# Expert rows divided 112 + 64 instead of 88 + 88, four result rows summed on TensorE, and the front of the middle stage done tile by tile, in a mixture-of-experts block on one Trainium2 core

## The reference

```python
x = x + attn(_layernorm(x), ...)            # 16 heads, 4 KV heads, causal, soft cap 50
x = x + ffn(_layernorm(x), ...)             # first expert stage
x = x + recur(_layernorm(x), Wa, Wx, ba, bx, Lam)
x = x + ffn(_layernorm(x), ...)             # second expert stage, same weights

def ffn(x, gate, Wg, Wu, Wd, Sg, Su, Sd):   # E = 64 experts, M = 176, capacity 96, top 6
    scores = softmax(x @ gate.T)            # the 3 best of 8 groups, then the 6 best experts
    slot = expert * 96 + min(place within the expert, 95)
    buf = zeros(E * 96, 256).at[slot].set(x[token]).reshape(E, 96, 256)
    g, u = einsum('ech,emh->ecm', buf, Wg), einsum('ech,emh->ecm', buf, Wu)
    out = einsum('ecm,ehm->ech', silu(g) * u, Wd)
    y = sum over the 6 choices of out[slot] * weight
    return y + silu(x @ Sg.T) * (x @ Su.T) @ Sd.T

def recur(x, Wa, Wx, ba, bx, Lam):          # h[t] = a[t] * h[t-1] + sqrt(1 - a[t]**2) * i[t] * x[t]
    r, i = sigmoid(x @ Wa.T + ba), sigmoid(x @ Wx.T + bx)
    a = exp(-8 * softplus(-Lam) * r)
    ...
```

## Time and profile before

| | |
|---|---|
| runs | 1285.45, 1286.99, 1289.58 us; median 1286.99 us |
| profiled execution | 1283.71 us, span 1281.9 us |
| busy, share of the span | PE 77%, PEld 46%, DVE 41%, ACT 57%, POOL 33% |
| stages | attention 0 to 623 us, first experts 692 to 845, middle 845 to 1085, second experts 1087 to 1240, end to 1282 |

### The profile page before, as it was taken

How to read it: one execution, slowest core, us unless ns; L and a number is a source line. 1 busy time by engine, 2 the same in 40 slices (tenths; PEclk the granted TensorE clock), 3 DMA queues, 4 the chain that set the end, 5 groups by cost and what they waited for, 6 DMA issues and landing times.

```text
span 1281.9 us, 18696 instructions
## 1 busy us (share of the span) xinstructions
PE 985.2 (77%) x6520; PEld 594.9 (46%) x6520; DVE 523.4 (41%) x1532; ACT 728.9 (57%) x960; POOL 423.7 (33%) x408
## 2 busy tenths in 40 slices
PE   4886868778887788787554999955587863999973
PEld 3633323322332323222334999943344442999962
DVE  7744431156221233230441333337776741333327
ACT  2285989999999999999101444414434400344420
POOL 3100000000222003234043565530098985556550
PEclk9878888998999998999686999976698976999985
DMA  9990000000111001100583999748133434899947
GB/s 352 394 393 31 1 1 1 1 17 1 42 47 37 17 16 60 39 20 6 148 254 92 292 295 289 177 118 273 50 116 117 123 109 106 243 293 284 261 72 305
DMA packets 94927, 176.11 MB, mean 137 GB/s; under 512 B 13119, under 2 KB 46880, under 8 KB 94833
## 3 DMA queue, kind: packets, MB, share of 16 engines
q1 hardware_dynamic: 58416, 130.55, 30.4%
q0 software_dynamic: 23616, 28.44, 10.4%
q10 hardware_dynamic: 12800, 15.93, 4.5%
HBM read 107.30 MB, written 83.72 MB: 149 GB/s over the span
## 4 chain that ended last, share of the span: by engine, by line
PE 32%; DVE 5%; DMA 3%; issue 3%; SPq 2%; POOL 2%; ACT 2%; DVEq 1%; POOLq 0%; ACTq 0%
PE PS L1323 13%; PE PS L1334 8%; PE PS L1261 4%; PE PS L1393 2%; PE PS L1310 2%; POOL expert_in L307 2%; SPq L1116 1%; DMA spare_space<-expert_out 1%; DMA normed<-xp 1%; SPq L1117 1%; PE PS L1246 1%; DMA XE<-expert_in 1%; PE PS L1270 1%; DMA expert_out<-ob,yidx 1%; POOL expert_out L1209 1%
## 5 line engine op out<-in xcount | busy, mean ns | idle before, releaser
L307 POOL DMA_INDIRECT expert_in<-xp,didx x192 | 192.9, 1005 | 621.7 <-ACT PR L684 483.9
L679 ACT ACTIVATE PR<-PS 128x1024 f32<-128x1024 f32 (+3 forms) x320 | 275.4, 935 | 55.7 <-PE PS L578 40.7
L684 ACT ACTIVATE PR<-PR 128x2048 f32<-128x2048 f32 (+3 forms) x160 | 272.4, 1705 | 0.0
L1209 POOL DMA_INDIRECT expert_out<-ob,yidx x128 | 180.6, 1411 | 148.2 <-ACT ob L1502 108.3
L587 PE MATMUL PS<-PR,V 128*32 128x512 f32 (+3 forms) x1280 | 164.8, 590 | 80.4 <-ACT PR L684 80.3
L575 PE MATMUL PS<-QT,KT 96*128 96x512 bf16 (+3 forms) x640 | 177.5, 372 | 19.8 <-ACT PR L679 16.9
L1740 DVE SCALAR_TENSOR_TENSOR gta<-gth,PS 88x192 f32<-88x192 f32 x128 | 44.8, 350 | 193.6 <-ACT gth L1492 193.6
L575 PEld LDWEIGHTS PS<-QT,KT 96*128 96x128 bf16 x640 | 59.3, 103 | 130.3 <-ACT PR L679 89.7
L1492 ACT ACTIVATE gth<-PS 88x192 f32<-88x192 f32 x128 | 41.7, 326 | 107.8 <-PE PS L1323 107.8
L1323 PEld LDWEIGHTS PS<-XT,spare_space 128*88 128x88 f32 x960 | 92.5, 164 | 8.8 <-issue 2.6
L1502 ACT ACTIVATE ob<-PS,wslot 96x256 f32<-96x256 f32 x128 | 60.1, 469 | 61.9 <-PE PS L1334 59.6
(11 more groups left out here) (257 smaller groups left out, 1355.3 us busy)
## 6 DMA issues: line engine op xcount, KB each, us to landing
spare_space<-in_wgu SPq DMA_DIRECT2D x60, 352.0 KB
expert_out<-zero SPq DMA_DIRECT2D x2, 8256.0 KB, 50.4
expert_in<-zero SPq DMA_DIRECT2D x2, 7776.0 KB, 39.3
XE<-expert_in ACTq DMA_DIRECT2D x32, 486.0 KB, 9.8
WGU<-in_wgu SPq DMA_DIRECT2D x44, 352.0 KB
spare_space<-expert_out SPq DMA_DIRECT2D x24, 512.0 KB, 6.1
spare_space<-in_wd SPq DMA_DIRECT2D x60, 176.0 KB
shared_space<-in_wgu SPq DMA_DIRECT2D x24, 352.0 KB
```

The costliest lines, as they stand in the source:

```text
L307: pool.indirect_dma_start(out=buf_d[f], out_offset=bass.IndirectOffsetOnAxis(ap=didx[b][:, r, j:j + 1], axis=0), in_=xp[b][:, r, :], in_of ...
L679: act.activation(PR[:, n % 3, 2 * pr:2 * pr + 2, cols(c, s):CW], PS[:, S0 + 2 * pr:S0 + 2 * pr + 2, cols(c, s):CW], ACT.Tanh, scale=1.0 / ...
L684: act.activation(PR[:, n % 3, :, lo:CW], PR[:, n % 3, :, lo:CW], ACT.Exp, scale=SOFT_CAP).then_inc(exp_done, 1)
L1209: pool.indirect_dma_start(out=y_d[f], out_offset=bass.IndirectOffsetOnAxis(ap=yidx[:, n % 4, j:j + 1], axis=0), in_=ob[:, i % EU, :], in_o ...
```

## The change

Three things are changed together. (1) The 176 middle rows of an expert are divided into 112 + 64. Gate a and up a are products with 112 weight columns; the last 64 rows of gate and of up are one product with 128 weight columns. That is six matmuls for each expert instead of eight. DVE's second instruction becomes two of 96 columns each, and the down weights are loaded by two DMAs (112 rows and 64 rows of 1 KB) instead of one of 88 rows of 2 KB. (2) The four result rows are summed on PE: the overflow product of each tile stays open and four products with the identity matrix add the four rows; DVE adds only the sum to X. The rows are awaited and released tile by tile. (3) Turning and copying of rows goes tile by tile (`turn_rows`, `turn_recur`: PE turns tiles 2 and 3 when ACT has copied tiles 0 and 1), and the order in the middle loop changes: `place` ahead of the sums on PE, and for c = 1 `slots` and `destinations` ahead of `recur_inputs` on DVE, with the statistics of two chunks taken one after the other. The last chunk of the end is added and stored in two halves.

```diff
-MH = M // 2
+MA = 112
+MB = M - MA
# loads on SP
-                sp.dma_start(wd, wd_d[e]).then_inc(loaded, 16)
+                sp.dma_start(wd[:, 0, :], wd_d[e, 0:MA, :]).then_inc(loaded, 16)
+                sp.dma_start(wd[0:MB, 1, :], wd_d[e, MA:M, :]).then_inc(loaded, 16)
# results on SP
-                if f == 0 and c:
-                    sp.wait_ge(results_free, c)
                 for r in range(CT):
                     i = CT * c + r
+                    if f == 0 and c:
+                        sp.wait_ge(result_psum, i - CT + 1)
# PE
-                    for j in range(4):
+                    for j, at, width in ((0, 0, MA), (2, MA, MA), (1, 2 * MA, 2 * MB)):
                         for hh in range(CH):
-                            last = pe.matmul(PS[0:MH, 4 + e % 2, j * CAP:(j + 1) * CAP], wgu[:, hh, MH * j:MH * (j + 1)],
+                            last = pe.matmul(PS[0:width, 4 + e % 2, j * CAP:(j + 1) * CAP], wgu[:, hh, at:at + width],
                                              XT[:, h % 2, e % EH, hh, :], start=(hh == 0), stop=(hh == CH - 1))
-            def overflow_rows(c):
+            def sum_rows(c):
                 ...
                 for r in range(CT):
-                    last = pe.matmul(PS[:, S0 + r // 2, (r % 2) * C:(r % 2 + 1) * C], WovT[...], O95[:], start=True, stop=True, ...)
-                last.then_inc(ov_psum, 1)
+                    acc = PS[:, S0 + r // 2, (r % 2) * C:(r % 2 + 1) * C] if c else PS[:, (S0, S0 + 1, A0, A0 + 1)[r], 0:C]
+                    pe.matmul(acc, WovT[...], O95[:], start=True, stop=False, ...)
+                    pe.wait_ge(y_ld[r], 16 * (c + 1))
+                    for j in range(NACC):
+                        last = pe.matmul(acc, const("ident"), GB[:, r, j * C:(j + 1) * C], start=False, stop=(j == NACC - 1), ...)
+                    last.then_inc(result_psum, 1)
             ...
+                    if r >= 2:
+                        pe.wait_ge(rowsT_ready, CT * n + r - 1)
             # the loop
                 if c < NC:
                     gates(c)
-                if c + 2 < NC:
-                    overflow_rows(c + 2)
                 if c:
                     place(k)
+                if c + 2 < NC:
+                    sum_rows(c + 2)
# ACT: one copy of each tile instead of one of all four
-                act.activation(xnT[:], PS[:, T0:T0 + 2, :], ACT.Copy).then_inc(rowsT_ready, 1)
+                for r in range(CT):
+                    act.wait_ge(rowsT_psum, CT * n + r + 1)
+                    act.activation(xnT[:, :, r * P:(r + 1) * P], PS[:, T0 + r % 2, ...], ACT.Copy).then_inc(rowsT_ready, 1)
# DVE, experts
-                    dve.scalar_tensor_tensor(ha[:, e % 2, :, :]..., bank[:, 2 * CAP:4 * CAP], 0.5, gta[:], ALU.mult, ALU.mult)
+                    dve.scalar_tensor_tensor(ha[:, e % 2, 0, :], bank[0:MA, 2 * CAP:3 * CAP], 0.5, gta[:, 0:CAP], ALU.mult, ALU.mult)
+                    dve.scalar_tensor_tensor(ha[0:MB, e % 2, 1, :], bank[MB:2 * MB, CAP:2 * CAP], 0.5, gta[0:MB, CAP:2 * CAP],
+                                             ALU.mult, ALU.mult).then_inc(act_ready, 1)
# DVE, statistics of chunk 0, tile by tile
+                        if (before, after) == (0, None):
+                            dve.wait_ge(result_psum, r + 1)
+                            added = dve.tensor_tensor(X[:, r, :], X[:, r, :], PS[:, (S0, S0 + 1, A0, A0 + 1)[r], 0:C], ALU.add)
             def add_results(c):
-                ...
-                dve.tensor_tensor(xc, xc, GB[:, :, 0:C], ALU.add).then_inc(results_free, 1)
+                dve.wait_ge(result_psum, CT * (c + 1))
+                dve.tensor_tensor(xc, xc, PS[:, S0:S0 + 2, :]..., ALU.add).then_inc(ov_added, 1)
# DVE, the loop
-                if c:
+                if c == 1:
+                    statistics(None, 0)
+                    statistics(2, None)
+                elif c:
                     statistics(c + 1 if c + 1 < NC else None, c - 1)
                 ...
-                if c == 1:
-                    add_results(3)
                 if c:
                     shift(k)
                     choose(k)
+                if c == 1:
+                    slots(k)
+                    destinations(k)
                 if c < NC:
                     recur_inputs(c)
                 if c + 2 < NC:
-                    add_overflow(c + 2)
+                    add_results(c + 2)
-                if c:
+                if c >= 2:
                     slots(k)
                     destinations(k)
# DVE combine_late and SP: the last chunk in two halves of two tiles, each stored when it is added
-                for r in range(CT):
+                for lo, hi in ((0, CT),) if c < NC - 1 else ((0, 2), (2, CT)):
```

More of the change, by code:

```diff
@@ L1048, in hybrid_kernel @@
         WD_space = keep("WD_space", [P, EU * 2 * C])
[L1049 removed]
+        WD = WD_space[0:MA, :].rearrange("p (e m c) -> p e m c", e=EU, m=2)
         XE = keep("XE", [CAP, 2, EH, RW])
         XT = keep("XT", [P, 2, EH, CH, CAP])
[L1052 to L1054 removed]
+        gth = keep("gth", [MA, 2, 2 * CAP])
+        gta = keep("gta", [MA, 2 * CAP])
+        ha = keep("ha", [MA, 2, 2, CAP])
         ob = keep("ob", [CAP, EU, C])
@@ L1077, in expert_weights @@
             loads = f * len(range(x, E, RING)) + e // RING + 1
-            return wgu, wd, ring_ld[x], 32 * loads
+            return wgu, wd, ring_ld[x], 48 * loads
         def last_user(x):
@@ L1178, in _ @@
                 results(1, c)
-            for c in range(NC):
+            for c in range(NC - 1):
                 sp.wait_ge(combined, c + 1)
                 sp.dma_start(x_rows[:, CT * c:CT * (c + 1), :], X[:, CT * c:CT * (c + 1), :]).then_inc(out_stored, 16)
-            sp.wait_ge(out_stored, 16 * NC)
+            for half in range(2):
+                i = CT * (NC - 1) + 2 * half
+                sp.wait_ge(combined, NC + half)
+                sp.dma_start(x_rows[:, i:i + 2, :], X[:, i:i + 2, :]).then_inc(out_stored, 16)
+            sp.wait_ge(out_stored, 16 * (NC + 1))
         @block.gpsimd
@@ L1332, in down @@
                     wd = expert_weights(f, e)[1]
-                    for m in range(2):
-                        last = pe.matmul(PS[0:CAP, 6 + e % 2, 0:C], ha[:, e % 2, m, :], wd[:, m, :],
+                    for m, width in enumerate((MA, MB)):
+                        last = pe.matmul(PS[0:CAP, 6 + e % 2, 0:C], ha[0:width, e % 2, m, :], wd[0:width, m, :],
                                          start=(m == 0), stop=(m == 1))
@@ L1375, in turn_recur @@
                     pe.wait_ge(xt_ready, NH)
[L1376 to L1379, removed]
+                for r in range(CT):
+                    if r < CT - 1:
+                        pe.wait_ge(recur_tile, (CT - 1) * c + r + 1)
+                    else:
+                        pe.wait_ge(xr_ready, c + 1)
+                    if r >= 2:
+                        pe.wait_ge(xrT_ready, CT * c + r - 1)
+                    for h in range(CH):
+                        at = (r // 2) * C + h * P
+                        last = pe.transpose(PS[:, T0 + r % 2, at:at + P], xr[:, r, h * P:(h + 1) * P], const("ident"))
+                    last.then_inc(xrT_psum, 1)
             def gates(c):
-                pe.wait_ge(xrT_ready, c + 1)
+                pe.wait_ge(xrT_ready, CT * (c + 1))
                 if c:
@@ L1414, in _ @@
             experts(0)
-            overflow_rows(0)
-            overflow_rows(1)
+            sum_rows(0)
+            sum_rows(1)
             turn_recur(0)
@@ L1453, in turned_rows @@
                 n = k - K0
-                act.wait_ge(rowsT_psum, n + 1)
                 if n:
                     act.wait_ge(shared_psum, n * SC)
-                act.activation(xnT[:], PS[:, T0:T0 + 2, :], ACT.Copy).then_inc(rowsT_ready, 1)
+                for r in range(CT):
+                    act.wait_ge(rowsT_psum, CT * n + r + 1)
+                    act.activation(xnT[:, :, r * P:(r + 1) * P],
+                                   PS[:, T0 + r % 2, (r // 2) * C:(r // 2 + 1) * C].rearrange("p (h n) -> p h n", h=CH), ACT.Copy)\
+                       .then_inc(rowsT_ready, 1)
             def scores(k):
@@ L1491, in gate @@
                         act.wait_ge(act_ready, i - 1)
-                    act.activation(gth[:, e % 2, :], PS[0:MH, 4 + e % 2, 0:2 * CAP], ACT.Tanh, scale=0.5).then_inc(gate_tanh, 1)
+                    act.activation(gth[:, e % 2, :], PS[0:MA, 4 + e % 2, 0:2 * CAP], ACT.Tanh, scale=0.5).then_inc(gate_tanh, 1)
                 def out(e):
@@ L1555, in turned_recur @@
                     act.wait_ge(gates_psum, 4 * c)
-                act.activation(xrT, PS[:, T0:T0 + 2, :], ACT.Copy).then_inc(xrT_ready, 1)
+                for r in range(CT):
+                    act.wait_ge(xrT_psum, CT * c + r + 1)
+                    act.activation(xrT[:, :, r * P:(r + 1) * P],
```

(2 more changed lines are left out.)

111 lines of the change are left out of this document (51 added, 60 removed).

## The result

The changed kernel took 1317.21 us (median of 4 runs, 1314.43 to 1323.63), the kernel before 1286.22 in the same comparison. The ratio is 1.025, with a 95% interval of 1.021 to 1.029: slower by some 31 us, and far outside the predicted range of 1256 to 1288. The profiled execution took 1315.19 us (span 1313.4), 31.5 us more than before's.

A forecast was written before the change was run, and what follows sets the result against it. PE bounds the expert stages, a chain of waits the middle stage's front, POOL its rest. Gains of 1.0 + 5.9 + 1.2 + 5.9 = 14.0 us take 1287.0 to 1273.0 us; range 1256 to 1288.

The forecast's parts named there:

- the down product takes 0.87 us in 4, 217 ns each: Expert stages: time of an expert's down product, 4 instructions with 256 moving columns, read from the trace before the change.
- the second rival: Expert stages: wide loads cost 110 ns on average, each stage at -1.0 to +1 us; 1286 us, chance 0.16.
- The load as the pace: Expert stages: weight loads bound gate and up, 8 at 97 ns and 4 at 111 ns, 1.22 us against 1.32.
- loads hidden: Rival for the expert stages: 96 moving columns stay the pace, each stage gains 19 to 21 us; 1245 us, chance 0.12.
- the division does nothing: The second rival's title: wide loads in the expert stages cancel the gain; 1286 us, within 0.3%, chance 0.16.
- DVE and DMA in the expert stages: Expert stages: DVE's extra instruction costs about 0.2 us behind the last expert only, the third weight DMA nothing.
- The front of K0: Before the first experts: tile-wise turning and copying lets `shift` move earlier; 1.0 us gained, bounds 0 and 1.2.
- The middle stage, k = 4: Front of the middle stage: sums at 8.7 us a chunk, row numbers for k = 4 come 1.2 us early.
- The rival with the lower clock: Middle stage: the clock stays at 1.2 GHz through the front, chunk 2's sums end 30 us later; 1303 us, chance 0.10.
- It holds, barely: Middle stage: k = 5 comes 1.9 us late against a slack of 3.4 - 1.2 us, so POOL need not wait.
- the slack of 3.4 us: Middle stage before the change: k = 5's row numbers are written at 964.76 us, POOL takes them at 968.37 us.
- The end, about nothing: End: two halves cost DVE about 0.6 us more, the last store is half as long; nothing, within 0.5 us.

The follow-up runs named there:

- pad_all: pad_down with the overflow product's WovT and O95 also padded with zeros from 64 to 128 rows; 1274.15 us, ratio to before 0.9911.
- pad_down: The changed kernel with the second down product zero-padded from 64 to 112 rows and its two weight transfers made one again; 1280.08 us, ratio to before 0.9954.
- pad_all_again: The same kernel as pad_all, timed again in a second comparison; 1278.45 us, ratio to before 0.9938.
- rows_88_72: The kernel before with the second down product summed over 72 of its 88 rows, nothing else changed; 1283.05 us (one run).
- division_padded: The kernel before with only the 112 + 64 division and the second down product zero-padded to 112 rows; 1272.23 us, ratio to before 0.9899.

## Why the prediction was wrong, step by step

- **The step that failed: "the down product takes 0.87 us in 4, 217 ns each" was carried over unchanged to a product over 64 rows.** The sum priced the wider loads of gate and up, and nothing for the fewer rows of the second down product. It takes 1.03 us, and gate and up behind it pay a second time, 1.40 instead of 1.22. That is 0.34 us an expert against a gain of 0.10: a loss of 0.24, or 15 us a stage, where the gain of 5.9 was forecast. My bounds did not hold it either: the second rival came nearest ("something that L1246 does not show"), but bounded it by 111 ns for every instruction, at +1 us, and looked at columns, not rows.
- **The trace of before had a row for it.** This is PEld's timeline at the end of the gates of c = 0, where the overflow product, with 64 rows, followed them:

```profile
881.20 0.19 PEld L1393 LDWEIGHTS PS<-spare_space,wab 128*128 128x128 f32 x1 [0.24 <-issue]
881.63 0.19 PEld L1393 LDWEIGHTS PS<-spare_space,wab 128*128 128x128 f32 x1 [0.24 <-issue]
882.57 1.59 PEld L1354 LDWEIGHTS PS<-O,WovT 64*128 64x128 f32 x8 [0.76 <-issue]
```

  The usual gap under products of 512 columns is 0.24 us; the load with 64 rows had 0.76, "<-issue". That the rows make the difference is shown by pad_all, where WovT has 128 rows at the same place and the gap is the usual one:

```profile
877.37 0.19 PEld L1368 LDWEIGHTS PS<-O,WovT 128*128 128x128 f32 x1 [0.24 <-issue]
```

  It was one crossing for eight instructions there, cheap enough to be overlooked. The change put it at every tile and at every expert.
- **The load as the pace, right.** The estimate of 97 and 111 ns, 1.22 us for 12 instructions, is what pad_down shows, to 0.01 us; the split into 97 and 111 ns was not measured by itself. With the down product padded, the stages gain 6.1 and 7.0 us (pad_down) against 5.9. The rivals "loads hidden" (1245 us) and "the division does nothing" (1286 us) are both out. The Trainium skill's rule for the duration of a load (TensorE: Matmul & The Clock Gate, section LDWEIGHTS) would have given 9 us a stage; the rows' own pace was nearer.
- **DVE and DMA in the expert stages, right.** DVE's second step lasts 0.26 us, and PE waited for it 4 times (2.4 us, in the list above). The lists of L1337 and L1348 name no DMA among what PE waited for.
- **The front of K0, right in size.** From ACT's small instruction at the end of `lambdas` to the first send it takes 26.4 us before (626.01 to 652.36), 25.0 in pad_all (626.43 to 651.46), 24.8 in pad_all_again and 24.0 in the changed kernel: 1.4 to 2.4 us less, against 1.0 forecast and a bound of 1.2.
- **The middle stage, k = 4: right but for the same cost.** I had the sums at 8.7 us a chunk and k = 4 sent 1.2 us earlier. Sums of 10.2 us made it 2.0 us later. With WovT padded it is sent 1.7 us earlier (79.7 against 81.4 us). The rival with the lower clock did not come: the clock in 845 to 928 us rose from 0.64 to 0.84.
- **"It holds, barely" for k = 5, wrong, crossings or not.** POOL waited 1.34 us, in the changed kernel and in both traces of pad_all. The row numbers of k = 5 came 37.7 us after those of k = 4 before and 41.4 us after them in pad_all: 3.7 us more, where the sum had 3.1 (1.2 + 1.9). And the slack of 3.4 us left out that POOL starts a send 0.9 us after its row numbers are written (918.35 to 919.22 us in pad_all). k = 4 to 7 took 151.8 us in pad_all where before had 149.9. But rows_88_72 and division_padded, which don't have this part of the change, took 151.2 us with no wait at k = 5, only with more of the longer sends (1.6 to 2.0 us instead of 0.98), so not all of the 1.9 us can be put down to the wait. In the end the middle stage gained nothing: 231.5 us against 231.3, where 1.2 us less were forecast.
- **The end, about nothing, right in the main**: 0.9 us shorter in the changed kernel and 0.2 to 0.8 in pad_all, but the traces of kernels with the old end differ among themselves by 0.7 us (38.9 to 39.6).

With the crossings gone, pad_all is 14.0 us shorter than before between the marks (1267.9 against 1281.9 of span), as the sum had it. That the total agrees so well is partly luck: the front (0.9 us) and the two stages (6.3 and 6.2 us) came out near their terms, the middle gave nothing, and the end and the stages made up for it. It is also one pair of executions; pad_all's two medians stand 11 and 6 us below those of the kernel before in the same comparisons. The cause of the loss is shown from both sides, by taking the crossings out of the changed kernel and by putting them into the kernel before. What happens inside PE at a crossing is not shown.

## What to carry to other kernels

Look at the number of rows of the weights, not only at the columns, when a product is divided: an uneven split that brought one part to 64 rows or fewer, amid products with more, cost two exposed loads each time (0.32 to 0.39 us together, in fp32), and zero rows that kept it above 64 cost PE nothing: the padded down product took 0.87 us, as the one with 88 rows did. In the list of loads, look for idle time "<-issue" ahead of one shape among others, and multiply it by how often the change will repeat it. A time taken from a row holds for the shape of that row; where the change alters any of its sizes, bound the new one from a row that shares that size.

## What was not expected of the hardware

- The crossing between weights of over 64 rows and of at most 64: 0.16 to 0.17 us each in the expert stages and 0.19 us in the sums, at the upper clock; the same for 64 and 32 rows, none for 72, 88 or 112 among 128.
- Leaving out 24 of 176 rows made the kernel before 44 us slower.
- The same program ran its attention in two ways, 8 us apart, at a granted clock of 0.92 and 0.87 in the same window.
